# Six layer norms with ScalarE's square root and VectorE's reciprocal, and matmuls of the unit matrix in TensorE's waits

## The chip, the cores and the metric

The kernel runs on one core of a Trainium2 chip. The metric is the time of one execution on the device in microseconds. Three executions of the kernel before took 1084.04, 1086.39 and 1088.76 us (median 1086.39 us). One further execution was profiled.

## What is computed

Six layers work on a residual `x` of 2 x 1024 tokens with 128 channels. Each layer normalises `x` over its channels and adds its result to the residual:

```python
x = x + 0.5 * L0_ffn(layernorm(x))        # 4-bit quantised SwiGLU, FF = 352
x = x + L0_attn(layernorm(x))             # gated delta rule, 16 heads of 8
x = x + 0.5 * L0_ffn(layernorm(x))
x = x + 0.5 * L1_ffn(layernorm(x))        # shared expert + 1 of 8 experts, inner 256
x = x + L1_attn(layernorm(x))             # causal softmax attention
x = x + 0.5 * L1_ffn(layernorm(x))

def layernorm(x, eps=1e-05):
    m = jnp.mean(x, axis=-1, keepdims=True)
    v = jnp.var(x, axis=-1, keepdims=True)
    return (x - m) / jnp.sqrt(v + eps)
```

## The kernel before, in words

`build_program` (L2080) runs six stages one after the other: `fp4_ffn` (tag `_f1`), `delta_attention` (`_d`), `fp4_ffn` (`_f2`), `moe_ffn` (`_m1`), `causal_attention` (`_c`), `moe_ffn` (`_m2`). The names in the trace leave the number out, so both feed-forward stages show as `_f` and both expert stages as `_m`. Each stage consists of one or more blocks. In a block every engine has an instruction list of its own, written out by hand; lists are held together by semaphores (`wait_ge`), and at the end of a block all engines meet. An engine works through its list strictly in order, and whatever stands in front of a wait on an engine delays all that stands behind it.

**The norm (class `Norm`, L92).** The residual stays on chip as 16 tiles of 128 tokens x 128 channels. VectorE (DVE) takes the statistics of the 16 tiles (L112), works out the mean and the variance with epsilon (L115 to L121, each 128 x 16), and raises `s_var`. GpSimd (POOL) waits for it and raises the variance to the power -0.5, using a tile `halfpow` full of -0.5 (L128; in the attention stage the same instruction stands at L1787). It raises `s_rstd`; DVE has nothing to do until then, and after it subtracts and multiplies tile by tile (L134), raising `s_xn` for each tile. TensorE (PE) waits for these and turns each tile over: it multiplies it with the unit matrix `k.ident`.

**What follows the norm.** In `fp4_ffn` DVE and POOL quantise four tiles at a time (L162 to L174) and PE turns them afterwards (`turn_x`, L359), then `gate_up` (L368). In `transposed_norm` (L448, the first block of the delta stage with a norm) PE turns the 16 tiles (L469) and ScalarE (ACT) copies them out (L477); the block after it, `delta_inputs`, has its projections at L619 with a Silu on ACT at L650. In `moe_front` (L1213) PE turns four tiles (`turn`, L1270), ACT copies them out (L1328), PE computes the router's logits (`route`, L1276, 8 columns for each tile) and the shared expert's first product (`gate_up(0, 0)`, L1291), and behind that `count` (L1284). From the logits DVE finds the expert of each token (L1354 onwards) and its place in a sorted list; POOL scatters the rows into DRAM by 16 indirect transfers (L1261), and SP (the queue of transfers) reads them back in six loads (L1252). Meanwhile PE goes on with the shared expert (L1291, L1301).

`moe_routed` (L1406) is the next block. PE reads the expert numbers of the first two slots, and then for each of 24 slots turns the rows (`to_columns`, L1443), multiplies by the expert's weights (L1449, 512 columns), turns the hidden values (L1457) and multiplies again (L1465).

In `causal_attention` (L1648 onwards) POOL has its power in the middle of setting up constants: it comes after the memsets and before `V`'s ones (L1788), the selector `c_sel` (L1789) and the masks. PE turns the tiles (L1958) and projects q and k (L1966); ACT and DVE split them in bf16 parts, which SP sends to DRAM (L1730) and fetches back. At the end of this stage PE waits until DVE has the reciprocal of the softmax's denominators (`s_rec`, L1891), spreads it over the heads (L2066) and projects the result (L2074).

## Time and profile before

| | |
|---|---|
| median of three executions | 1086.39 us (1084.04 to 1088.76) |
| the profiled execution | 1078.19 us, of which the span from first to last instruction is 1076.5 us |
| PE busy | 736.8 us, 68% |
| DVE busy | 716.9 us, 67% |
| POOL busy | 411.6 us, 38% |
| ACT busy | 340.5 us, 32% |
| mean granted clock of PE | 0.855 of full |

No engine is busy all the time: the stages have different limits, and at the seams between them most engines stand idle in turn.
### The profile page before, as it was taken

The page shows a single profiled execution, that of the slowest core. Times are in us where ns is not written, and L with a number is a line of the kernel's source. Part 1 is how long each engine was busy: PE and PEld are TensorE (multiplying, and loading weights), DVE is VectorE, ACT ScalarE, POOL GpSimd, SP SyncE. Part 2 cuts the span into 40 slices and gives each one's busy share as a digit, 9 for nine tenths or more (in the row PEclk, how much of TensorE's full clock was granted, in tenths as well). Part 3 has the DMA queues.
Part 4 walks back from the last instruction along what each step waited for, and adds up shares of the span by engine and source line. Part 5 has one row for each costly group of instructions (what it writes and reads, how often), then busy time and mean ns, then how long its engine had stood idle before and what let it go on. Part 6 is the DMA issues. An engine that isn't in the chain of part 4 may idle for free. (4 is left out here: it accounts for less than half of the span.)

```text
span 1076.5 us, 15238 instructions
## 1 busy us (share of the span) xinstructions
PE 736.8 (68%) x5421; PEld 493.0 (46%) x5421; DVE 716.9 (67%) x1203; ACT 340.5 (32%) x579; POOL 411.6 (38%) x593
## 2 busy tenths in 40 slices
PE   0575145877775999836658792468787777738794
PEld 0354121477665998614455461233333333236462
DVE  7996484689996888389934234578887888244232
ACT  0211064000001550011211250417666666702152
POOL 3353100278886960034424254022333322302343
PEclk9987586689998999858958895759999999976897
DMA  7000000000000000030000212757100000000303
GB/s 180 0 1 1 11 0 0 1 1 1 2 1 1 2 2 1 15 117 1 1 0 31 79 41 73 244 97 114 28 8 9 8 9 8 7 3 13 89 32 106
DMA packets 42881, 35.89 MB, mean 33 GB/s; under 512 B 6167, under 2 KB 37336, under 8 KB 42808
## 3 DMA queue, kind: packets, MB, share of 16 engines
q1 hardware_dynamic: 40248, 29.61, 11.6%
q0 software_dynamic: 2560, 5.31, 1.5%
q8 instruction: 45, 0.74, 0.3%
q14 instruction: 28, 0.23, 0.1%
HBM read 17.45 MB, written 15.89 MB: 31 GB/s over the span
## 5 line engine op out<-in xcount | busy, mean ns | idle before, releaser
L1881 DVE TENSOR_REDUCE blockmax<-c_bank 128x8 f32<-128x1024 f32 x144 | 175.0, 1223 | 47.7 <-PE c_bank L2007 41.4
L1944 ACT ACTIVATE PT<-c_bank 128x1024 f32<-128x1024 f32 x144 | 145.5, 1025 | 71.8 <-PE c_bank L2029 71.7
L2043 PE MATMUL c_bank<-PT,V 128*9 128x256 f32 (+3 forms) x960 | 78.7, 431 | 14.5 <-POOL PT L1833 10.5
L798 PE MATMUL sums<-prod,ident 128*128 128x128 f32 x512 | 69.0, 293 | 27.0 <-DVE prod L824 27.0
L2000 PE MATMUL c_bank<-KA,QA 48*128 48x128 bf16 (+3 forms) x608 | 59.9, 282 | 36.0 <-DMA KA<-qk_parts_dram 16.2
L1833 POOL TENSOR_SCALAR_AFFINE_SELECT PT<-PT 128x256 f32<-128x256 f32 x128 | 49.1, 408 | 81.1 <-ACT PT L1944 81.0
L798 PEld LDWEIGHTS sums<-prod,ident 128*128 128x128 f32 x512 | 63.7, 203 | 32.2 <-DVE prod L824 32.2
L1539 POOL DMA_INDIRECT routed_results<-results_m,rows_m x48 | 46.0, 957 | 66.6 <-DVE results_m L1516 64.8
L2029 PE MATMUL c_bank<-QA,KA 51*128 51x128 bf16 (+3 forms) x480 | 56.8, 302 | 17.0 <-DMA QA<-nrows 16.5
L368 PE MATMUL gu_f<-gu_wT,xqT_f 128*128 128x352 f32 x128 | 52.8, 567 | 17.9 <-DVE h_f L298 17.9
L1522 DVE TENSOR_TENSOR r_h_m<-r_silu_m,r_gu_m 128x256 f32<-128x256 f32 x48 | 20.2, 421 | 66.9 <-ACT r_silu_m L1507 66.9
L1449 PE MATMUL r_gu_m<-m_gu,rowsT_m 128*128 x96 | 55.4, 661 | 1.8 <-ACT rowsT_m L1493 1.8
L754 POOL TENSOR_TENSOR decayed<-decayed,outer 128x512 f32<-128x512 f32 x32 | 40.6, 1269 | 32.8 <-DVE outer L843 32.8
L2000 PEld LDWEIGHTS c_bank<-KA,QA 48*128 48x128 bf16 x608 | 24.2, 97 | 59.5 <-ACT PT L1944 31.7
L171 POOL TENSOR_TENSOR q_yh_f<-q_yh_f,q_magich_f 128x704 f32<-128x704 f32 x16 | 26.8, 1676 | 60.7 <-DVE q_yh_f L168 57.1
L1261 POOL DMA_INDIRECT sorted_rows<-xs_m,where_m x32 | 31.0, 970 | 47.5 <-DVE where_m L1382 38.4
L783 ACT COPY s<-sums 128x64 f32<-128x64 f32 x32 | 6.8, 213 | 133.5 <-DVE wt L840 133.5
L368 PEld LDWEIGHTS gu_f<-gu_wT,xqT_f 128*128 128x128 f32 x128 | 28.9, 237 | 35.3 <-issue 28.5
L1815 POOL COPY negmax<-runmax 128x8 f32<-128x8 f32 x16 | 3.1, 193 | 108.6 <-DVE runmax L1886 108.6
L2043 PEld LDWEIGHTS c_bank<-PT,V 128*9 128x9 f32 x960 | 23.7, 90 | 43.6 <-issue 18.0
L2029 PEld LDWEIGHTS c_bank<-QA,KA 51*128 51x128 bf16 x480 | 16.3, 94 | 57.3 <-issue 28.4
L824 DVE TENSOR_TENSOR prod<-hist,keys 128x1024 f32<-128x1024 f32 x30 | 36.6, 1220 | 5.7 <-PE keys L790 3.0
(320 smaller groups left out, 1801.8 us busy)
## 6 DMA issues: line engine op xcount, KB each, us to landing
sorted_rows<-blank SPq DMA_DIRECT2D x2, 1584.0 KB, 14.0
rows_m<-sorted_rows SPq DMA_DIRECT2D x12, 264.0 KB, 4.7
qk_parts_dram<-qk_parts SPq DMA_DIRECT2D x8, 384.0 KB, 3.4
QA<-qk_parts_dram SPq DMA_DIRECT2D x6, 384.0 KB, 8.0
KA<-qk_parts_dram SPq DMA_DIRECT2D x6, 384.0 KB, 9.7
back_m<-routed_results SPq DMA_DIRECT2D x8, 256.0 KB, 3.7
qk_parts_dram<-qk_parts SPq DMA_DIRECT2D x8, 256.0 KB, 3.2
m_gu<-in_rt_gate SPq DMA_DIRECT2D x1, 1024.0 KB, 6.0
```

Source lines behind the costliest of these rows:

```text
L368: ins = nc.tensor.matmul(gu[:, s, m, 0:FF], xt, k.gu_wT[:, m * FF:(m + 1) * FF], start=True, stop=True)
L754: nc.gpsimd.tensor_tensor(decayed[:, kind], decayed[:, kind], outer1[:, kind], ALU.add).then_inc(s_added[kind], 1)
L798: ins = nc.tensor.matmul(sums[:, kind, 0], k.ident[:, :], prod[:, kind, e // HALF, :, e % HALF, :], start=(e == 0), stop=(e == DH - 1))
L824: nc.vector.tensor_tensor(prod[:, kind].rearrange("p a t e n -> p a t (e n)"), state.to_broadcast([P, 2, 2, HALF * NC]), keys[:, p % 2].re ...
L1449: nc.tensor.matmul(gu[:, j % 2, :], rowsT[:, j % 2, :], moe.gu[:, bass.ds(owner[j], 1), :], start=True, stop=True).then_inc(s_gu, 1)
L1539: nc.gpsimd.indirect_dma_start(out=result_dram[:, :], out_offset=bass.IndirectOffsetOnAxis(ap=rows[:, j, D:D + 1].bitcast(I32), axis=0), i ...
L1833: ins = nc.gpsimd.affine_select(out=diag, in_=diag, compare_op=ALU.is_ge, fill=0.0, base=0, pattern=[[0, BATCH], [1, P]], channel_multipli ...
L1881: nc.vector.tensor_reduce(blockmax[:, h % 2, :, HALFQ * n:HALFQ * (n + 1)], slot_of((1, m)).rearrange("p b (n c) -> p b n c", c=P), AX.X, ...
L1944: nc.scalar.activation(PT[:, u % PRING, :, :], slot_of((0, u)), ACT.Exp, scale=SCALE).then_inc(s_pt, 1)
L2000: ins = nc.tensor.matmul(out[:, b, n * P:end * P], QA[at, h, PLACE[i] * P:(PLACE[i] + 1) * P], KA[at, h, spot * P:(spot + end - n) * P], s ...
L2029: ins = nc.tensor.matmul(out[:, b, o:o + n], KA[at, h, PLACE[j] * P:(PLACE[j] + 1) * P], q, start=True, stop=True)
L2043: ins = nc.tensor.matmul(O[32 * g:32 * g + DH + 1, f * P:f * P + n], V[:, b, j, h, :], PT[:, u % PRING, b, o:o + n], start=(j == 0), stop= ...
```

## The change

It has two parts. First, in all six norms ACT takes the square root of the variance, after loading the table for it at the start of the block, and DVE takes the reciprocal; POOL's power and the tile `halfpow` are gone. Where another ACT table is needed afterwards it is loaded right behind the root (Silu in `fp4_ffn`, Sigmoid in `moe_front`). Second, `keep_busy` issues f32 matmuls of the unit matrix with itself (512 columns) into a bank of PSUM that is overwritten later. They wait for nothing and nothing waits for them: they stand in PE's list in front of work. There are 9 ahead of `turn_x(0, 0)` in `_f2`, 4 ahead of the turning in `_d`, 4 ahead of `turn(0)` and 2 behind the last `down` in the front of `_m1` and of `_m2`, 2 ahead of `to_columns(0)` in each routed block, 4 ahead of the wait for the weights in `_c`, and 9 ahead of its wait for `s_rec`: 42 in all.

```diff
+def keep_busy(k, bank, count):
+    for _ in range(count):
+        k.nc.tensor.matmul(bank, k.ident[:, :], k.ident[:, :].unsqueeze(1).to_broadcast([P, BANK // P, P]), start=True, stop=True)
...
-    def on_gpsimd(self, pool):
-        nc = self.nc
-        nc.gpsimd.memset(self.halfpow[:, :], -0.5).then_inc(self.s_half, 1)
-        pool.wait_ge(self.s_half, 1)
-        pool.wait_ge(self.s_var, 1)
-        nc.gpsimd.tensor_tensor(self.rstd[:, :], self.var[:, :], self.halfpow[:, :], ALU.pow).then_inc(self.s_rstd, 1)
+    def on_scalar(self, act):
+        act.preload_act_table(ACT.Sqrt)
+        act.wait_ge(self.s_var, 1)
+        self.nc.scalar.activation(self.std[:, :], self.var[:, :], ACT.Sqrt).then_inc(self.s_std, 1)
+
+    def on_vector_rstd(self, dve):
+        dve.wait_ge(self.s_std, 1)
+        self.nc.vector.reciprocal(self.rstd[:, :], self.std[:, :]).then_inc(self.s_rstd, 1)
...  fp4_ffn, TensorE and ScalarE
                 if prepare:
                     prepare.on_tensor(pe)
+                else:
+                    keep_busy(k, y[:, 0, :], 9)
                 turn_x(0, 0)
...
+                ln.on_scalar(act)
+                act.preload_act_table(ACT.Silu)
...  transposed_norm, TensorE
+                keep_busy(k, tp[:, 3, :], 4)
                 for t in range(TILES):
                     pe.wait_ge(ln.s_xn, t + 1)
...  moe_front, TensorE (start and end) and ScalarE
+                keep_busy(k, y[:, 0, :], 4)
                 turn(0)
...
+                keep_busy(k, logits[:, :], 2)
...
+                ln.on_scalar(act)
                 act.preload_act_table(ACT.Sigmoid)
...  moe_routed, TensorE
                 owner = {0: expert_of(0), 1: expert_of(1)}
+                keep_busy(k, y[:, 1, :], 2)
                 to_columns(0)
...  causal_attention, GpSimd
-                pool.wait_ge(s_set, 3)
-                pool.wait_ge(ln.s_var, 1)
-                nc.gpsimd.tensor_tensor(ln.rstd[:, :], ln.var[:, :], ln.halfpow[:, :], ALU.pow).then_inc(ln.s_rstd, 1)
                 nc.gpsimd.memset(V[:, :, :, :, DH:DH + 1].rearrange("p b j h a -> p (b j h a)"), 1.0).then_inc(s_set, 1)
...  causal_attention, TensorE
+                keep_busy(k, bank[:, 7, :], 4)
                 pe.wait_ge(s_w, 6 * 16)
                 turn_tiles(0)
...
+                keep_busy(k, bank[:, 4, :], 9)
                 pe.wait_ge(s_rec, 1)
```

## Rows read from the trace of the kernel before

**Rows 1.** Line 134, what ended its engine's idle time: us in total, times.
```profile
  POOL rstd_f L128: 6.2, 2
```
**Rows 2.** Timeline of all engines, front of `_m1`: start us, us, engine, line.
```profile
549.39 1.28 ACT L1325 ACT_TABLE_LOAD   x1 [4.27 <-PEq L85]
...
553.56 0.17 DVE L121 TENSOR_SCALAR var_m<-ln_tmp_m 128x16 f32<-128x16 f32 x1
553.88 2.90 POOL L128 TENSOR_TENSOR rstd_m<-var_m,halfpow_m 128x16 f32<-128x16 f32 x1 [4.38 <-DVE var_m L121]
556.82 4.19 DVE L134 TENSOR_SCALAR xn_m<-residual,mean_m,rstd_m 128x128 f32<-128x128 f32 x16 [3.09 <-POOL rstd_m L128]
...
557.22 2.27 PE L1270 MATMUL sh_gu_m<-ident,xn_m 128*128 128x128 f32 x8 [9.12 <-DVE xn_m L134]
558.50 0.59 ACT L1328 COPY xnT_m<-sh_gu_m 128x512 f32<-128x512 f32 x1 [7.83 <-PE sh_gu_m L1270]
```
**Rows 3.** Timeline of `_m1`: ACT takes a 128x16 function from DVE.
```profile
567.81 0.29 DVE L1354 TENSOR_REDUCE top_m<-logits_m 128x16 f32<-128x128 f32 x1 [6.81 <-PE logits_m L1276]
568.13 0.22 ACT L1330 ACTIVATE score_m<-top_m 128x16 f32<-128x16 f32 x1 [3.03 <-DVE top_m L1354]
```
**Rows 4.** Timeline of `_f1`: the smallest reciprocal on DVE.
```profile
22.56 0.35 DVE L164 RECIPROCAL q_invx_f<-q_scalex_f 128x32 f32<-128x32 f32 x1
```
**Rows 5.** Timeline of PE in `_m1`: router, then 512-column matmuls early and late.
```profile
564.27 3.42 PE L1276 MATMUL logits_m<-m_router,xnT_m 128*128 128x8 f32 x16
567.54 3.76 PE L1291 MATMUL sh_gu_m<-xnT_m,m_shared_gu 128*128 128x512 f32 x4
...
592.05 3.60 PE L1291 MATMUL sh_gu_m<-xnT_m,m_shared_gu 128*128 128x512 f32 x8
```
**Rows 6.** Timeline of PE in `_d`: the first work after 22.75 us of rest.
```profile
128.91 4.17 PE L469 MATMUL ntp_d<-ident,xn_d 128*128 128x128 f32 x16 [22.75 <-DVE xn_d L134]
```
**Rows 7.** Windows: stretch, length, busy us of PE, PEld, DVE, ACT, POOL, PEclk, DMA.
```profile
132.00:132.50 0.50, 0.50 (x4) 0.32 (x3) 0.50 (x3) 0.26 (x1) 0.00 (x0) 0.69 0.00 0
572.00:573.00 1.00, 1.00 (x3) 0.48 (x3) 0.77 (x3) 0.00 (x0) 0.00 (x0) 0.69 0.00 0
989.00:990.00 1.00, 1.00 (x6) 1.00 (x6) 0.73 (x4) 0.00 (x0) 0.70 (x2) 0.53 0.00 0
```
**Rows 8.** Timeline from the end of the front of `_m1` into its routed block.
```profile
597.05 2.05 PE L1301 MATMUL sh_y_m<-m_shared_down,sh_hT_m 128*128 128x128 f32 x16 [1.41 <-DVE sh_hT_m L1345]
597.52 3.13 SPq L1252 DMA_DIRECT2D rows_m<-sorted_rows  x6
...
602.64 0.33 PE L1443 MATMUL r_tpx_m<-ident,rows_m 128*128 128x128 f32 x1 [3.54 <-issue]
...
603.42 2.07 PE L1449 MATMUL r_gu_m<-m_gu,rowsT_m 128*128 x2 [0.45 <-ACT rowsT_m L1493]
...
611.23 1.06 PE L1449 MATMUL r_gu_m<-m_gu,rowsT_m 128*128 x2
...
612.91 1.06 PE L1449 MATMUL r_gu_m<-m_gu,rowsT_m 128*128 x2
```
**Rows 9.** Timeline of the front of `_c`: the norm, POOL's constants, first projections, first transfers.
```profile
668.29 5.50 DVE L134 TENSOR_SCALAR xn_c<-residual,mean_c,rstd_c 128x128 f32<-128x128 f32 x16 [3.13 <-POOL rstd_c L1787]
668.63 1.03 POOL L1789 COPY c_sel<-ident 128x1024 f32<-128x1024 f32 x1
...
671.79 3.53 PE L1966 MATMUL c_bank<-xnT_c,c_wqkv 128*128 128x512 f32 x4
...
677.46 17.72 SPq L1730 DMA_DIRECT2D qk_parts_dram<-qk_parts  x24
```
**Rows 10.** Timeline of PE at the end of `_c`.
```profile
950.75 5.76 PE L2066 MATMUL c_bank<-c_rec,c_sel 128*128 128x256 f32 x16 [9.34 <-DVE c_rec L1891]
...
956.35 0.83 PE L2074 MATMUL c_bank<-c_wp,YT 128*128 128x128 f32 x6
```
**Rows 11.** Timeline of PE in `_f2`: its first work.
```profile
469.09 1.11 PE L359 MATMUL htp_f<-ident,xq_f 128*128 128x128 f32 x4 [16.70 <-POOL xq_f L174]
```

More of the change, by code:

```diff
@@ L101, in __init__ @@
         self.rstd = k.sb(f"rstd{tag}", [P, TILES], ctx=ctx)
-        self.halfpow = k.sb(f"halfpow{tag}", [P, TILES], ctx=ctx)
+        self.std = k.sb(f"std{tag}", [P, TILES], ctx=ctx)
         self.xn = xn if xn is not None else k.sb(f"xn{tag}", [P, TILES, D], ctx=ctx)
         self.s_var = k.sem(f"s_var{tag}")
-        self.s_half = k.sem(f"s_half{tag}")
+        self.s_std = k.sem(f"s_std{tag}")
         self.s_rstd = k.sem(f"s_rstd{tag}")
@@ L310, in _ @@
                 ln.on_vector_stats(Chain(dve, s_ldve))
+                ln.on_vector_rstd(dve)
                 ln.on_vector_apply(dve, 0, XTILES)
@@ L343, in _ @@
                     moe.on_gpsimd(k, pool)
-                ln.on_gpsimd(pool)
                 for g in range(XG - 1):
@@ L458, in _ @@
                 ln.on_vector_stats(Chain(dve, s_dve))
+                ln.on_vector_rstd(dve)
                 ln.on_vector_apply(dve)
-            @block.gpsimd
-            def _(pool):
-                ln.on_gpsimd(pool)
             @block.tensor
             def _(pe):
+                keep_busy(k, tp[:, 3, :], 4)
                 for t in range(TILES):
@@ L1256, in _ @@
             def _(pool):
-                ln.on_gpsimd(pool)
                 pool.wait_ge(s_xs, 2)
@@ L1321, in _ @@
                             gate_up(c + 1, half)
+                keep_busy(k, logits[:, :], 2)
             @block.scalar
             def _(act):
+                ln.on_scalar(act)
                 act.preload_act_table(ACT.Sigmoid)
@@ L1391, in _ @@
                 ln.on_vector_stats(Chain(dve, s_ndve))
+                ln.on_vector_rstd(dve)
                 ln.on_vector_apply(dve)
@@ L1775, in _ @@
                 nc.gpsimd.memset(ones[:, :], 1.0).then_inc(s_ones, 1)
-                nc.gpsimd.memset(ln.halfpow[:, :], -0.5).then_inc(s_set, 1)
                 nc.gpsimd.memset(zeros[:, :], 0.0).then_inc(s_set, 1)
@@ L1790, in _ @@
                     [P, DH, HEADS, DH])).then_inc(s_set, 1)
-                pool.wait_ge(s_set, 5)
+                pool.wait_ge(s_set, 4)
                 for n, base in enumerate((0, HALFP, -HALFP)):
@@ L1796, in _ @@
                                             pattern=[[-1, P]], channel_multiplier=1).then_inc(s_set, 1)
-                pool.wait_ge(s_set, 11)
+                pool.wait_ge(s_set, 10)
                 for n, t in enumerate((idm, future)):
@@ L1801, in _ @@
                         nc.gpsimd.tensor_copy(t[at, s, :], shifted[at, 3 * n + shift, :]).then_inc(s_set, 1)
-                pool.wait_ge(s_set, 19)
                 def add_bias():
@@ L1849, in _ @@
                 ln.on_vector_stats(Chain(dve, s_ldve))
+                ln.on_vector_rstd(dve)
                 ln.on_vector_apply(dve)
@@ L1866, in _ @@
                 low(NQK - 1)
-                dve.wait_ge(s_set, 4)
+                dve.wait_ge(s_set, 3)
                 for g in range(4):
@@ L1912, in middle @@
                     nc.scalar.copy(parts[:, n % RING, 1, :], rest[:, n % RING, :]).then_inc(s_mid, 1)
+                ln.on_scalar(act)
                 act.wait_ge(s_w, 6 * 16)
@@ L1982, in _ @@
                 pe.wait_ge(s_rest, NQK)
-                pe.wait_ge(s_set, 19)
+                pe.wait_ge(s_set, 18)
                 def group_of(h):
```

## The prediction

> **What bounds the kernel now.** I read the page's share of busy time first: PE 68% and DVE 67%, so nothing bounds the whole, and the seams have to be read one by one. Then what ended the idle time ahead of line 134: POOL's power does, twice for 6.2 us in all in the feed-forward stages [rows 1]. Three more lines of that answer hold the other four norms with 3.1 us each. So at six seams DVE stands still for 3.1 us, and the timeline of one seam shows that all others stand still with it: PE's first turn comes 0.40 us after DVE's first tile, with 9.12 us of rest before it [rows 2]. Last come the windows with PEclk. In `_m1` PE rests through the norm, then works from 557.22 us, and the clock rises to full only within 572 to 573 us [rows 2, 7]. In that time it works at half speed on the way to the experts' choice. The same holds in the front of `_c`, at its end, and in the routed blocks.
>
> **Part 1, the norms.** Removed from each seam: the 3.12 us between the variance's end and the first tile (3.09 to 3.13 in the rows) [rows 1, 2, 9]. Added: a hand-over from DVE to ACT, 0.03 us (568.10 to 568.13), and a 128x16 function, 0.22 us, a Sigmoid standing in for the root [rows 3]; a hand-over back, taken as 0.03 us as well; the reciprocal of 128x16, at most the 0.35 us of the 128x32 one, at least the 0.17 us of the 128x16 instruction before the power, and I take 0.25 us as half the elements lie between [rows 2, 4]; and DVE's own wait for it, 0.04 us. That is 0.57 us, with bounds 0.45 and 0.8 us. Each seam gains 2.55 us, six gain **15.3 us** (13.9 to 16.0). Nothing else is late at the variance: PE, ACT and POOL wait for this chain.
>
> The table loads of the root stand at the block's start, where the Sigmoid's load stood: 1.28 us from 549.39, done long before the variance at 553.73 [rows 2]. The second load moves behind the root. In `_m` the root ends 0.32 us ahead of the first tile, the load 0.96 us behind it, and ACT's first copy came 1.68 us behind it: hidden by 0.7 us [rows 2]. If that cover were gone it would cost up to 1.28 us in each `_m` and less in the others. The Trainium skill ("ScalarE: Activation LUTs", What ACT_TABLE_LOAD costs) gives 2.66 us for every switch with its drain; by that the copy would be 0.66 us late in each `_m`, 1.3 us in the sum. No row here shows a drain.
>
> In `_c` POOL no longer holds its constants back until the power is done. The 16 tiles took 5.50 us there against 4.19 us in `_m`, because the 1.03 us copy of `c_sel` ran beside the first one [rows 2, 9]. It now runs beside the statistics: **1.2 us** (0 to 1.3).
>
> **Part 2, what a matmul of the unit matrix costs.** Its kind is L1291, 512 columns in f32. Four records, that is two matmuls, take 3.76 us at 1.2 GHz, and eight records, four matmuls, 3.60 us at 2.4 GHz [rows 5]; without the tail of the last, 1.71 and 0.86 us each. All 42 are 72 us cold and 36 us warm, so almost all must lie under waits. What they bring is clock. Whether they raise it: two dense cold matmuls and little more raised it in `_m1` (from 567.54 to within 572 to 573) [rows 5, 7]. A start at block begin should therefore be warm after some 3 to 5 us.
>
> The four ahead of the norm's turns (`_d`, `_m1`, `_m2`, `_c`) have 549.39 to 557.22 less 2.55, that is 5.28 us of cover [rows 2]. With two cold and two warm they take 5.1 us: hidden. All cold they take 6.84 us and overrun by 1.56 us. What the clock then gives:
> - `_d`: nothing; DVE paces the turns at 0.26 us, and the clock is full before the projections anyway [rows 6, 7].
> - `_m` fronts: from 557 us to the counts come 32 router records (16 of them in 3.42 us [rows 5], so 6.84 us) and two cold matmuls of 512 columns. At full clock throughout, 3.4 and 1.7 us go, 5.1 us. At the least nothing does. The question is whether the clock stays up through work of 8 columns: in `_m1` this work, cold and unbroken, did not raise it [rows 5, 7], and in `_m2` the clock fell within 989 to 990 us with PE busy throughout, after a short rest [rows 7]. I take it to hold for the first part only and to be lost before the last 16 records: 1.7 us, nearer the row that fell. Two stages: **3.4 us** (0 to 10.2).
> - `_c` front: the first two projections are dense and come at once; they go from 1.71 to 0.86 us each, and SP's transfers, which run without a break from 677.46 us for 17.7 us, start that much sooner [rows 9]: **1.7 us** (0 to 1.8).
>
> The nine in `_f2` have until 469.09 less 2.55; PE has rested since 452.39 (16.70 us before), and with some 2 us for the meeting of the engines that leaves 12 us of cover, of which a run half cold takes 10 [rows 11]. What follows there is a chain on DVE with a turn only now and then; I count 0 (0 to 0.7).
>
> The nine at the end of `_c` have 9.34 us [rows 10]. PE comes out of the heads' work at 2.4 GHz, so they take 7.7 us and keep it. The eight matmuls at L2066 took 950.75 to 956.35, 5.6 us, and take 8 x 0.43 = 3.4 us warm: **2.2 us** (0 to 2.2).
>
> The two pairs around the experts' seam are the doubtful ones. PE's last work in the front ended at 599.10, SP's issues at 600.65 [rows 8]. A warm pair ends at 600.81 and holds the block back by 0.2 us; a cold one to 602.52, by 1.9 us. The pair ahead of `to_columns(0)` stands plainly on the path, since PE's rest before the first turn is put down to its own issue and not to a transfer [rows 8]: 1.7 us warm, 3.4 us cold. It buys the first three slots at full clock: 603.42 to 611.23 is 7.81 us against three times 1.68 us (611.23 to 612.91), 2.8 us [rows 8]. Net 2.8 - 1.7 - 0.2 = 0.9 us in each, **1.8 us** (minus 7 to plus 2).
>
> **The sum.** 15.3 + 1.2 + 3.4 + 1.7 + 2.2 + 1.8 = 25.6 us. The profiled execution took 1078.19 us (span 1076.5, 1.7 around it), so it would come to 1052.6 us. That execution was 8.2 us faster than the median of the three shown; I take the same difference off the median: 1086.4 - 25.6 = 1060.8, rounded to **1061 us**.
>
> **The rivals.**
> *The clock holds through the fronts.* The `_m` fronts give 5.1 us each in place of 1.7: 6.8 us more, 1054 us. For it: PE no longer rests there. Against it: the fall at 989 us.
> *The clock is lost again before the work.* The matmuls then only cost. The norms' 15.3, 1.2 for `c_sel` and 2.2 at the end of `_c` stay; the experts' seams cost 2 x (2.5 + 0.2): 13.3 us, 1073 us. For it: at that seam PE still rests, from the first pair's end to the second pair, for some 1.9 us. In `_d` 16 plain turns raised the clock within 132.0 to 132.5 us, with PE at rest for 22.75 us before [rows 6, 7]. The Trainium skill ("TensorE: Matmul & The Clock Gate", Part 4) says that turning does not count as busy for the clock; by that rule every front would lose its clock during the turns, as this rival has it. The row of `_d` disagrees, so I give the rival no more than a fifth.
> *Slower than before: the matmuls stay cold and overrun their waits.* At a price p each, the overruns are 4 x (4p - 5.28) ahead of the turns, 2 x (2p - 1.55) behind the fronts, 4p in the routed blocks and 9p - 9.34 at the end of `_c`, that is 33p - 33.5. At p = 1.71 it is 22.9 us, against 16.5 us from the norms and `c_sel`: 1093 us. It decides from p = 1.51 us on. Against it: dense matmuls raised the clock wherever they ran for 5 us.
> *The root's chain is no shorter.* If the table load came behind the wait for the variance, 1.28 us would stand in each chain: 7.7 us less gain, 1069 us. Against it: the Sigmoid's preload ran at block start [rows 2].
>
> **How the numbers follow.** Forecast 50%, clock holds 19%, clock lost 22%, slower 4%, root's chain 5%. The range of 1051 to 1074 us takes in all but the slower case and the tails of the two outer ones. A change of 0.5% is 5.4 us, about what a measurement of this kernel can tell from none. Faster by more: 93%; within: 3%; slower: 4%.
>
> **What would show it.** ACT's root and DVE's reciprocal within 0.6 us between variance and first tile, six times; table loads at block starts. In `_m`, PEclk 1.00 in the turns and 0.50 before the last router records (lost) or 1.00 up to the counts (holds). In the routed block, L1449 at 1.68 us from the first slot, and its first turn 1.9 us later after SP's last issue than before. At the end of `_c`, L2066 in 3.5 us. Wrong at once: unit-matrix records of 0.85 us in the routed block, a PE still on them when the first tile is ready, or a gap of 3 us left ahead of line 134.

## The result, and the profile after

| | before | after | ratio |
|---|---|---|---|
| median | 1085.28 us (four executions) | 1058.30 us (four executions, 1056.38 to 1061.64) | 0.9749, 95% interval 0.9722 to 0.9777 |
| profiled execution | 1078.19 us, span 1076.5 | 1056.38 us, span 1054.7 | |

The forecast was 1061 us, 25.6 us less than before. The medians differ by 27.0 us, the two profiled executions by 21.8 us. Why these two numbers disagree turned out to be a question of its own (below).

The page of the changed kernel: busy time of each engine, and PE's granted clock in forty slices.

```profile
span 1054.7 us, 15405 instructions
...
PE 762.8 (72%) x5505; PEld 498.4 (47%) x5505; DVE 717.7 (68%) x1209; ACT 349.2 (33%) x591; POOL 392.9 (37%) x581
...
PEclk9987687699997999877969997759999999997997
```

PE is busy for 26.0 us longer than before and the kernel is over 20 us shorter. The clock's mean rose from 0.855 to 0.887.

The norm's chain in `_m1`, from the timeline of all engines (start us, us, engine, line; it answers to [rows 2]):

```profile
539.17 1.28 ACT L130 ACT_TABLE_LOAD   x1 [4.28 <-PEq L85]
...
539.20 5.89 PE L95 MATMUL sh_y_m<-ident 128*128 128x512 f32 x8 [1.33 <-PEq L85]
...
543.34 0.17 DVE L127 TENSOR_SCALAR var_m<-ln_tmp_m 128x16 f32<-128x16 f32 x1
543.55 0.21 ACT L132 ACTIVATE std_m<-var_m 128x16 f32<-128x16 f32 x1 [3.10 <-DVE var_m L127]
...
543.78 1.28 ACT L1338 ACT_TABLE_LOAD   x1
543.80 0.25 DVE L136 RECIPROCAL rstd_m<-std_m 128x16 f32<-128x16 f32 x1 [0.28 <-ACT std_m L132]
...
545.62 0.58 ACT L1341 COPY xnT_m<-sh_gu_m 128x512 f32<-128x512 f32 x1 [0.56 <-PE sh_gu_m L1280]
```

From the variance's end (543.51) to the first tile (544.09) it is 0.58 us, where it was 3.09 us [rows 2]. The table of the next function is loaded behind the root, ends at 545.06, and the copy comes 0.56 us later: hidden. The reciprocal of 128x16 takes 0.25 us. All six norms look like this (0.57 us each).

PE in the same stretch, then its granted clock (windows: stretch, length, busy us of PE, PEld, DVE, ACT, POOL, PEclk, DMA):

```profile
544.93 1.68 PE L1280 MATMUL sh_gu_m<-ident,xn_m 128*128 128x128 f32 x8
...
549.02 2.17 PE L1286 MATMUL logits_m<-m_router,xnT_m 128*128 128x8 f32 x16
551.04 3.38 PE L1301 MATMUL sh_gu_m<-xnT_m,m_shared_gu 128*128 128x512 f32 x4
```
```profile
542.00:543.00 1.00, 1.00 (x3) 0.48 (x2) 0.93 (x8) 0.00 (x0) 0.00 (x0) 0.50 0.00 0
543.00:544.00 1.00, 1.00 (x2) 0.32 (x2) 0.65 (x5) 0.43 (x2) 0.00 (x0) 0.67 0.00 0
544.00:545.00 1.00, 1.00 (x4) 0.40 (x3) 0.96 (x5) 1.00 (x1) 0.00 (x0) 1.00 0.00 0
...
548.00:550.00 2.00, 2.00 (x21) 2.00 (x20) 0.27 (x2) 1.11 (x2) 0.00 (x0) 1.00 0.04 8
550.00:552.00 2.00, 2.00 (x9) 1.52 (x10) 0.62 (x3) 0.35 (x2) 0.00 (x0) 0.62 0.00 0
552.00:554.00 2.00, 2.00 (x4) 0.93 (x3) 1.93 (x5) 1.15 (x1) 0.00 (x0) 0.52 0.02 4
554.00:556.00 2.00, 2.00 (x9) 1.04 (x8) 1.97 (x4) 0.60 (x1) 0.00 (x0) 1.00 0.00 0
```

The clock comes up before the first turn and stays up through all turns and nearly all router records (2.17 us for 16, before 3.42 [rows 5]). It falls at 550.5 us, as the dense products begin, with PE busy since 539.20 us. PE goes from the multiplications into the turns without a rest.

To locate gains and losses I cut all executions at the same rows and took the differences of their starts. Each column is one profiled execution in us; "changed" is the kernel just shown, after_again the same kernel on another chip, before_again the kernel before on that chip; the others are the experiments below. R is the first row of DVE that reads `psR`, behind the delta stage's scan. The stretches between those of the table are left out, so the rows don't add up to the span. The longest of them, in `_c` from SP's first store to `c_rec`, took 271.5 to 275.3 us, in an order that doesn't go with the edits.

| from, to | before | before_again | norms_only | busy_only | changed | after_again | seam_moved | best |
|---|---|---|---|---|---|---|---|---|
| start, first tile of `_f1` | 20.47 | 20.20 | 17.79 | 20.29 | 17.84 | 17.75 | 18.07 | 17.72 |
| first tile of `_d`, R | 219.64 | 217.41 | 221.91 | 220.10 | 216.27 | 219.08 | 219.75 | 219.02 |
| R, first tile of `_f2` | 113.56 | 113.50 | 110.95 | 113.50 | 110.94 | 110.96 | 111.02 | 110.95 |
| `_m1`: first tile, router's maxima | 10.99 | 10.98 | 10.99 | 10.91 | 7.22 | 7.41 | 7.29 | 7.10 |
| `_m1`: SP's loads of rows, first turn of rows | 5.12 | 5.17 | 7.88 | 13.42 | 10.16 | 7.16 | 5.82 | 6.31 |
| `_m1`: first turn of rows, SP's loads of results | 50.72 | 52.12 | 50.59 | 47.86 | 47.87 | 47.96 | 48.88 | 48.39 |
| `_c`: first tile, SP's first store | 9.17 | 8.24 | 8.33 | 9.33 | 6.58 | 6.60 | 6.58 | 6.60 |
| `c_rec`, first tile of `_m2` | 20.32 | 20.68 | 17.38 | 18.28 | 15.77 | 15.78 | 15.77 | 15.78 |
| `_m2`: first tile, router's maxima | 10.99 | 10.99 | 10.99 | 10.91 | 10.93 | 6.95 | 10.92 | 6.94 |
| `_m2`: SP's loads of rows, first turn of rows | 5.97 | 4.92 | 8.38 | 11.14 | 11.18 | 7.03 | 5.37 | 5.38 |
| `_m2`: first turn of rows, SP's loads of results | 50.66 | 50.81 | 50.54 | 47.99 | 47.94 | 47.98 | 47.98 | 47.88 |
| span | 1076.5 | 1075.2 | 1066.4 | 1083.5 | 1054.7 | 1046.5 | 1052.8 | 1044.4 |

### The profile page after: what moved, and what is told of

Its sections match the earlier page's. It is cut to its first block and busy times, and to the rows that moved or that the text cites. A ratio compares the mean times of both kernels' runs of the same rounds, so it can differ in the third digit from the quotient of the medians.

```text
span 1054.7 us, 15405 instructions
## 1 busy us (share of the span) xinstructions
PE 762.8 (72%) x5505; PEld 498.4 (47%) x5505; DVE 717.7 (68%) x1209; ACT 349.2 (33%) x591; POOL 392.9 (37%) x581
## 5 line engine op out<-in xcount | busy, mean ns | idle before, releaser
L376 PE MATMUL gu_f<-gu_wT,xqT_f 128*128 128x352 f32 x128 | 50.5, 546 | 17.9 <-DVE h_f L306 17.8
L1463 PE MATMUL r_gu_m<-m_gu,rowsT_m 128*128 x96 | 50.3, 605 | 2.2 <-ACT rowsT_m L1508 2.2
L2042 PEld LDWEIGHTS c_bank<-QA,KA 51*128 51x128 bf16 x480 | 16.4, 94 | 57.0 <-issue 28.2
L393 PE MATMUL y_f<-down_wT,hqT_f 128*128 128x128 f32 (+1 forms) x192 | 30.8, 320 | 13.2 <-ACT hqT_f L431 13.2
```

The source lines that it names most:

```text
L376: ins = nc.tensor.matmul(gu[:, s, m, 0:FF], xt, k.gu_wT[:, m * FF:(m + 1) * FF], start=True, stop=True)
L1463: nc.tensor.matmul(gu[:, j % 2, :], rowsT[:, j % 2, :], moe.gu[:, bass.ds(owner[j], 1), :], start=True, stop=True).then_inc(s_gu, 1)
L2042: ins = nc.tensor.matmul(out[:, b, o:o + n], KA[at, h, PLACE[j] * P:(PLACE[j] + 1) * P], q, start=True, stop=True)
```

## The experiments

They ran in three groups of four, each group on one chip with the kernel before beside it. The medians of the kernel before on these chips were 1083.95, 1077.36 and 1078.33 us, so kernels of different groups are compared by their ratios.

### First group: the two parts alone, the pairs, and _m2's front

**norms_only**, all seven calls of `keep_busy` removed from the changed kernel, of which one is shown:

```diff
...
-                keep_busy(k, y[:, 0, :], 4)
...
```

> The changed kernel without any multiplication of the unit matrix: its norms (ACT's root, DVE's reciprocal) and the new order of the constants in _c stay. Theory A (the sum of the prediction, its terms checked on the trace after): six norms at 2.54 us and 1.1 us for the copy of c_sel, 16.4 us less than before, ratio 0.985; the clock at the fronts, the end of _c and in the routed blocks as before. Rival B: most of the gain comes from the shorter chains, with the clock following by itself from PE's shorter rests; then 20 us or more, ratio 0.981 or less. On the late ACT function in the shared expert (a rest of 7.14 us ahead of the last pair of Silus in _m1, some 2.5 us more than the pace asks): theory A puts it down to ACT's longer program, so it is here as well; if it comes from PE's added instructions it is absent here. The 3.8 us that the delta stage gave between 160 and 212 us without any edit in it: if they hang on how far the stages' start is shifted against the clock, they can be here in any size, and no theory forecasts them.

Measured: 1067.26 us, ratio 0.9846 (0.9831 to 0.9861), 16.7 us less. Theory A forecast 16.4 us. The table shows the norms alone: 2.7 us at `_f1`, 2.6 us at `_f2`, and the fronts of `_m1` and `_m2` at 10.99 us as before. The clock doesn't follow by itself, so rival B falls. The profile of this kernel has the late Silus told of below, which is part of why it is only 10.1 us shorter than that of the kernel before.

**busy_only**, the kernel before plus the same seven calls:

```diff
...
+                keep_busy(k, y[:, 0, :], 4)
                 turn(0)
...
```

> The kernel before with all 42 multiplications of the unit matrix and none of the rest: GpSimd's power stays, with the order of _c's constants. Theory A: the multiplications give what the after trace shows of them, some 4 in the front of _m1, 1 to 2 in _m2's, 1.8 in _c's front, 2.0 at the end of _c, less 0.7 in each routed block's seam: 7 to 8 us less than before, ratio 0.993; the norms' chains take 3.12 us as before, and ACT's Silus in the shared expert keep the pace they had before (no 7 us rest). Rival C (the rests of PE are 2.5 us longer here than in the changed kernel, so the clock is lost again between multiplications and turns): ratio 0.998 or more, with a granted clock of 0.50 in the router's records of both _m stages.

Measured: 1088.17 us, ratio 1.0038 (1.0022 to 1.0053): 4.2 us *slower* than before. Theory A (7 to 8 us faster) falls, and rival C holds in a stronger form. The fronts of `_m1`, `_m2` and `_c` take what they took before. PE in the front of `_m1`, and its clock:

```profile
549.99 6.53 PE L95 MATMUL sh_y_m<-ident 128*128 128x512 f32 x8 [1.33 <-PEq L85]
557.79 2.27 PE L1279 MATMUL sh_gu_m<-ident,xn_m 128*128 128x128 f32 x8 [1.27 <-DVE xn_m L140]
```
```profile
557.00:558.00 1.00, 0.21 (x1) 0.14 (x1) 0.61 (x3) 0.00 (x0) 0.35 (x1) 1.00 0.00 0
558.00:559.00 1.00, 1.00 (x5) 0.55 (x4) 1.00 (x5) 0.08 (x1) 0.00 (x0) 1.00 0.00 0
559.00:560.00 1.00, 1.00 (x6) 0.74 (x5) 1.00 (x6) 0.51 (x1) 0.00 (x0) 0.58 0.00 0
```

GpSimd's power holds the first tile back, PE rests for 1.27 us, and the clock falls some 1.4 us behind the first turn, before it has bought anything. In the changed kernel the shorter norm closes that rest. That the rest is what loses the clock is argued from this pair of profiles and not shown: further down, a rest of 1.6 us in `_m2` lost it in some executions and not in others. At `_m1`'s experts' seam the clock was down as well: the last `down` took 3.79 us (2.05 before), the pair behind it 2.91 us, and the first turn of rows came 13.4 us behind SP's loads. What did pay is 2.0 us at the end of `_c` and 2.9 and 2.7 us in the routed blocks. The rows name where 4.2 us can be lost; they don't add up to exactly that number, because no profile of the kernel before exists from this chip.

**no_seam_pairs**, the two pairs around the experts' seam removed:

```diff
-                keep_busy(k, logits[:, :], 2)
...
-                keep_busy(k, y[:, 1, :], 2)
```

> The changed kernel without the two pairs at the experts' seams (2 at the front's end, 2 ahead of the first turn of rows, in each _m). The prediction had the pairs bring 0.9 us net in each stage: by that this kernel is 1.8 us slower than the changed one. Theory A (the trace after): each pair stands on the path with 1.7 to 1.9 us, 3.5 us in all, and they bring 2.8 us of pace in the first three slots: this kernel is 0.8 us faster in each stage, 1.6 us in all, and its first turn of rows comes 3.5 us sooner behind PE's last matmul of the shared expert (5.4 us now, 1.9 to 3.5 us here), with the first three slots at 2.6 us apart as before. If ACT's late Silu in the shared expert is still there (rest of 7 us), it doesn't come from these pairs.

Measured: 1060.80 us, ratio 0.9790 (0.9768 to 0.9813). In its `_m1` the first turn of rows comes 7.89 us behind SP's loads (10.16 in the changed kernel), but from there to the loads of results it takes 50.60 us (47.87). So the pairs cost 2.3 us there and bring 2.7 us, 0.4 us net where Silus are late. In its `_m2` the turn comes only 0.7 us sooner (10.44 against 11.18) and the block takes 2.6 us longer (50.54 against 47.94), 1.9 us net. Theory A had 3.5 us for the cost and falls; in time the pairs can't be told from nothing here.

**m2_six**, six multiplications in `_m2`'s front, with `out` handed on to `moe_front`:

```diff
-                keep_busy(k, y[:, 0, :], 4)
+                keep_busy(k, y[:, 0, :], 6 if out is not None else 4)
```

> The changed kernel with six instead of four multiplications ahead of the turns in _m2 alone (_m1 keeps four). In the changed kernel the four ran warm there, ended 1.6 us ahead of the first turn, and the clock fell at the first turns and stayed at 0.50 for 14 us; in _m1, where the four ran cold and PE had no rest before its turns, it stayed full until the router was nearly done. Theory A (the rest loses the clock): with six there is no rest, the clock holds through most of the router as in _m1, and the span from first normalised tile to the router's maxima falls from 10.9 to about 7.2 us: 3.7 us faster than the changed kernel, ratio to before 0.9715. Rival B (the turns and the 8-column matmuls lose it, whenever they come): the clock falls within 2 us of the same place, and the time is the changed kernel's within 0.5 us.

Measured: 1057.87 us, ratio 0.9780 (0.9755 to 0.9805). First tile to maxima took 8.96 us: the clock fell 4.4 us behind the first tile, where it fell 1.3 us behind it in the changed kernel, not at the same place as rival B has it, and theory A's 7.2 us wasn't reached either. The third group settles how much this says.

### The late Silus

In all four kernels of this group, and in the changed kernel as first profiled, ACT comes late near the end of the shared expert, with nothing waited for that the trace shows. The changed kernel:

```profile
573.38 0.60 ACT L1348 ACTIVATE sh_silu_m<-sh_gu_m 128x512 f32<-128x512 f32 x1 [1.12 <-PE sh_gu_m L1301]
...
580.38 3.13 SPq L1263 DMA_DIRECT2D rows_m<-sorted_rows  x6
581.13 1.08 ACT L1348 ACTIVATE sh_silu_m<-sh_gu_m 128x512 f32<-128x512 f32 x2 [7.14 <-PE sh_gu_m L1301]
```

The rest should be 4.58 us; it is 7.14 us, and the function comes 0.75 us behind SP's first load. In the kernel before the last Silu (595.68) is earlier than that load (597.52). PE's last `down` and the whole seam are late with it. The next two kernels ask whether the edit does this.

### Second group

**small_ones**, the kernel before with 42 matmuls of one column ahead of `_f2`'s turns:

```diff
+                else:
+                    for _ in range(42):
+                        nc.tensor.matmul(y[:, 0, 0:1], k.ident[:, :], k.ident[:, 0:1], start=True, stop=True)
                 turn_x(0, 0)
```

> The kernel before with 42 matmuls of one column each (unit matrix times its first column) in PE's wait ahead of _f2's turns: as many instructions as the change adds to PE, some 0.05 to 0.1 us each, far too short to bring the clock up or to overrun that wait. Asks where the late Silus of the shared expert come from: all four kernels run so far show ACT's 5th and 7th Silu late in both _m stages, the 7th only 0.8 to 1.5 us behind SP's first load of rows, so 3 to 4 us late; the kernel before doesn't. Theory D (the place of the code: what comes later in the program lies elsewhere, and ACT's instructions arrive late there): the late Silus appear here too, and the time is 2 to 5 us above before's. Rival E (something the multiplications or the norms do in the _m stages themselves): Silus at before's pace, first load of rows 1.7 us or more behind the last Silu, time that of before within 1 us.

Measured: 1078.17 us, ratio 1.0001 (0.9986 to 1.0015), and no late Silu. Their price was mis-sized: 84 records took 18.05 us, 0.21 us each and two to a matmul. They did overrun the wait: the first turn came 10.49 us behind the first tile, 7.38 us before. The next wait swallowed it, for `gate_up` began at 14.84 us behind that tile, as before. Theory D would fall, but nothing in this whole group had a late Silu, so the run says less than it should.

**late_scatter**, the changed kernel with POOL's scatters held back:

```diff
                 pool.wait_ge(s_where, 1)
+                pool.wait_ge(s_silu, NB * HALVES)
```

> The changed kernel with GpSimd's sixteen scatters held back until ACT's eighth Silu is done, so that no scatter runs beside the shared expert. Asks whether the scatters make ACT late. If they do (ACT's late instructions come over the same transfer engines): Silus 5 to 8 keep the pace of 1.7 and 5.2 us by turns, with the last some 14 us behind the third; the kernel as a whole is some 14 to 20 us slower in each _m, because the rows are loaded later. If not: a rest of ACT of 7 us and more with nothing waited for stays ahead of the last pair, at the same place in its program.

Measured: 1094.60 us in one execution. The Silus keep their pace, and the loads of rows come 50.3 us behind the maxima in place of 29.1, so 21 us later in each `_m` and not 14 to 20. Since no kernel of this group was late, it doesn't show that the scatters are the cause. It stays open.

**no_d_f2**, without the four in `_d` and the nine in `_f2`:

```diff
-                    keep_busy(k, y[:, 0, :], 9)
...
-                keep_busy(k, tp[:, 3, :], 4)
```

> The changed kernel without the four multiplications in _d and without the nine in _f2; the other 29 stay. The prediction counted both at nothing: then this kernel's time is the changed kernel's (ratio to before 0.975). Rival F (the four in _d shift PE's clock in the delta stage: three executions with them gained 0.5 to 3.4 us between the first normalised tile of _d and the end of the scan, the two with the norms alone or with the old norms lost 0.5 to 2.3 us): 3 to 5 us slower than the changed kernel, ratio 0.978 to 0.980, with the loss between 160 and 350 us. The nine in _f2 give nothing in either.

Measured: 1055.67 us, ratio 0.9790 (0.9764 to 0.9817). By the ratio that is where rival F puts it. By the rows it isn't: from the first tile of `_d` to R it took 217.65 us, inside the range of kernels that have the four (216.3 to 219.8).

**seam_moved**, the same two pairs at other places:

```diff
                 for c in range(NB):
+                    if c + 1 == NB:
+                        keep_busy(k, logits[:, :], 2)
                     down(c)
...
-                keep_busy(k, logits[:, :], 2)
...
+                keep_busy(k, y[:, 1, :], 2)
                 owner = {0: expert_of(0), 1: expert_of(1)}
-                keep_busy(k, y[:, 1, :], 2)
```

> The changed kernel with its two pairs at the experts' seam moved, none removed: the pair on logits goes ahead of the shared expert's last down (where PE waits 2.9 us for ACT and DVE), the pair on y goes ahead of the two loads of expert numbers into PE's registers, not behind them. Theory A (each pair stood on the path with 1.7 to 1.9 us, and the register loads of 1.9 us run beside matmuls that are already issued): first turn of rows 3.5 us sooner after PE's last matmul of the shared expert (2 to 3.5 us in place of 5.4), pace of 1.68 us from the first slot kept: 2.5 to 3.5 us faster in each _m, 5 to 7 us in all, ratio 0.969. Rival G (PE's rest behind the block's end loses the clock, or the register loads wait for the matmuls anyway): the y pair still delays the turn by its own 1.7 us; 2 us faster or less.

Measured: 1049.91 us, ratio 0.9727 (0.9698 to 0.9756). PE at the seam of its `_m1`:

```profile
584.10 1.95 PE L1311 MATMUL sh_y_m<-m_shared_down,sh_hT_m 128*128 128x128 f32 x16
588.00 2.45 PE L95 MATMUL r_y_m<-ident 128*128 128x512 f32 x4 [1.95 <-PEq L1258]
590.24 0.42 PE L1458 MATMUL r_tpx_m<-ident,rows_m 128*128 128x128 f32 x1
```

The first turn comes 4.19 us behind the last `down` (5.42 us in no_d_f2, where the pairs have their old places), and in `_m2` 3.44 us. The register loads do run beside the pair. Against SP's loads the gain is 1.2 and 1.7 us. In `_m1` 1.0 us of it goes again, because the clock fell during the pair (48.88 us in the routed block instead of 47.9). So the truth lies between theory A and rival G.

### Third group: the same kernels on one chip

**after_again** and **before_again** are the two kernels unchanged, so they have no diff.

> The changed kernel as it is, on the same chip as the next three, to read them against it. Also for the late Silus: they showed in all four kernels of one group of runs and in none of the four of another, so neither the norms nor the multiplications decide it. If they go with the chip, all four of this group show them in both _m stages or none does; if with the kernel, this one shows them (it did in its first profile) and no_d_f2, which differs from it before _m1 alone, does not. Ratio to before 0.975 to 0.979. First normalised tile to the router's maxima 7.2 us in _m1 and 10.9 in _m2, in _c first tile to SP's first store 6.6, first turn of rows to SP's first load of results 47.9 us.

> The kernel before as it is, for one more profile. Its profile shown at the start took 1078 us where its timed runs took 1084 to 1089, and on two other chips its median was 1084 and 1077 us. If the late Silus go with the chip, they are here exactly when the other three of this group have them, with the first turn of rows 7.9 us behind SP's first load in place of 5.1, and a time 5 to 6 us above 1077; if they go with the kernel, they are absent here whatever the others show.

Measured: after_again 1048.20 us, ratio 0.9731 (0.9704 to 0.9758); before_again 1076.94 us in one execution. No Silu was late in any of the four, and the changed kernel is among them. Its ratio is just outside the 0.975 to 0.979 expected, because `_m2`'s front took 6.95 us and not 10.9. The same program had late Silus on one chip and none on another, so the edit by itself doesn't bring them; they go with the chip or with what a group shares. Whether the kernel before has them on those chips too, no profile shows. Where changed kernels showed them, the median of the kernel before was 1085.28 and 1083.95 us; where they didn't, 1077.36 and 1078.33. They cost 2.8 us in `_m1` and at least 2.4 us in `_m2` (7.88 and 8.38 us in norms_only against 5.12 and 5.97 us; before_again took 4.92 us in `_m2`, which makes it 3.5). It fits that the timed runs of before had them too and its profiled execution didn't, which would explain 21.8 us in the profiles against 27.0 in the medians. No profile of the kernel before shows them, so this stays an inference. On this chip the profiles differ by 28.7 us (1075.2 - 1046.5) and the medians by 30.1 us.

**no_d**, without the four in `_d` alone:

```diff
-                keep_busy(k, tp[:, 3, :], 4)
```

> The changed kernel without the four multiplications in _d; the nine in _f2 stay. Forecast of the prediction: nothing, ratio equal to after_again's within its interval. Rival F (they shift PE's clock in the delta stage): 3 us or more slower than after_again, lost between 160 and 350 us. Against F so far: from the first normalised tile of _d to the first carry behind the scan five profiles with the four took 216.3 to 219.8 us, the two with new norms without them 217.7 and 221.9, so that a difference of the two means of 2 us stands beside a spread of 3.5 us.

Measured: 1052.64 us, ratio 0.9745 (0.9720 to 0.9771), 4.4 us above after_again with overlapping intervals. In the profile `_d` to R took 221.32 us. Seven profiles of changed kernels with the four took 216.3 to 219.8 us (mean 218.0), busy_only 220.1; the three changed kernels without them took 217.7, 221.3 and 221.9 us. That leans to rival F with some 2 us, but executions of the kernel before, also without them, took 217.4, 218.1 and 219.6 us. The scatter is as large as the effect: not settled.

**best**, the edits of seam_moved and m2_six together:

```diff
-                keep_busy(k, y[:, 0, :], 4)
+                keep_busy(k, y[:, 0, :], 6 if out is not None else 4)
...
+                    if c + 1 == NB:
+                        keep_busy(k, logits[:, :], 2)
                     down(c)
...
-                keep_busy(k, logits[:, :], 2)
...
+                keep_busy(k, y[:, 1, :], 2)
                 owner = {0: expert_of(0), 1: expert_of(1)}
-                keep_busy(k, y[:, 1, :], 2)
```

> The changed kernel with the two pairs moved (as in seam_moved) and six multiplications ahead of _m2's turns (as in m2_six). From the rows of those two: 1.2 to 1.9 us at each experts' seam (first turn of rows 5.4 to 5.8 us behind SP's first load instead of 7.0 where no Silu is late), up to 1 us lost again in a stage whose clock falls during the y pair, and 2.0 us in _m2's front (9.0 us in place of 10.9): 3 to 5 us less than after_again, ratio to it 0.995 to 0.997. If the gains are swallowed by what is late next, its time is after_again's.

Measured: 1046.39 us, ratio 0.9703 (0.9687 to 0.9719), the fastest kernel of all. The seams gave 0.9 and 1.7 us against after_again (6.31 and 5.38 against 7.16 and 7.03). `_m2`'s front gave nothing: 6.94 us with six against 6.95 with four. 1.8 us between the medians, with overlapping intervals, is less than the 3 to 5 us expected. In the profile of after_again the four already did what six were meant to do.

That makes `_m2`'s front the most instructive stretch. The same four multiplications, ending 1.61 us ahead of the first turn both times; first the changed kernel, then after_again:

```profile
944.00:946.00 2.00, 0.45 (x2) 0.28 (x2) 1.61 (x9) 1.37 (x2) 0.00 (x0) 1.00 0.00 0
946.00:948.00 2.00, 2.00 (x10) 1.48 (x9) 2.00 (x10) 0.85 (x3) 0.00 (x0) 0.61 0.00 0
948.00:950.00 2.00, 2.00 (x11) 2.00 (x11) 1.34 (x6) 0.45 (x1) 0.00 (x0) 0.50 0.00 0
...
958.00:960.00 2.00, 2.00 (x5) 0.97 (x4) 1.97 (x1) 0.39 (x1) 0.00 (x0) 0.50 0.00 0
960.00:962.00 2.00, 2.00 (x6) 0.73 (x5) 1.50 (x6) 0.20 (x1) 0.00 (x0) 0.98 0.00 0
```
```profile
944.00:946.00 2.00, 0.39 (x3) 0.16 (x2) 1.58 (x9) 1.20 (x2) 0.00 (x0) 1.00 0.00 0
946.00:948.00 2.00, 2.00 (x12) 1.30 (x11) 2.00 (x9) 1.00 (x3) 0.00 (x0) 1.00 0.00 0
948.00:950.00 2.00, 2.00 (x20) 2.00 (x21) 1.52 (x6) 1.06 (x2) 0.00 (x0) 1.00 0.00 0
950.00:952.00 2.00, 2.00 (x20) 2.00 (x19) 0.00 (x0) 0.59 (x1) 0.00 (x0) 1.00 0.00 0
952.00:954.00 2.00, 2.00 (x5) 0.96 (x5) 1.58 (x7) 1.38 (x2) 0.00 (x0) 0.61 0.00 0
954.00:956.00 2.00, 2.00 (x7) 1.18 (x6) 2.00 (x1) 0.72 (x2) 0.00 (x0) 0.54 0.00 0
956.00:958.00 2.00, 1.83 (x5) 0.52 (x4) 1.83 (x8) 0.14 (x1) 0.00 (x0) 1.00 0.00 0
```

In the one the clock falls among the turns at about 946.4 us and stays down for nearly 14 us; in the other it falls at 952.4 us, when the dense matmuls begin, and is back 3.4 us later. That is 4.0 us of difference with one and the same program. So a rest of 1.6 us doesn't lose the clock every time. It may still make it likelier: of the seven profiles with four multiplications and this rest, the clock fell within 0.9 to 1.5 us of the first turn in five, after 3.8 us in no_d and after 6.7 us in after_again; in the two with six and no rest (m2_six and best) it fell after 4.0 and 6.5 us. What six bring over four stays open.

## Why the prediction was right, point by point

| term of the sum | forecast us | measured us | from |
|---|---|---|---|
| six norms | 15.3 | 15.2 | 2.52 to 2.56 in each, between variance and first tile, changed against before |
| `c_sel` in `_c` | 1.2 | 1.1 of DVE, 0.8 of the front | 16 tiles in 4.40 us instead of 5.50; first tile to SP's first store 9.17 to 8.33, before to norms_only |
| fronts of `_m` | 3.4 | 3.8, and 7.6 on the third chip | 10.99 to 7.22 in `_m1`; 10.99 to 10.93 or 6.95 in `_m2`, each to the router's maxima |
| front of `_c` | 1.7 | 1.7 | 8.33 to 6.6, norms_only to changed |
| `_f2` | 0 | 0 | 110.95 us with and without |
| `_d` | 0 | 0 to 2 | not settled |
| end of `_c` | 2.2 | 1.6 to 2.0 | 17.38 to 15.77; 20.32 to 18.28 |
| experts' seams | 1.8 | 1.4 without late Silus; minus 4.7 in the changed kernel's own profile | 2.0 us later, 2.7 us shorter, twice; 5.0 and 5.2 us later, 2.9 and 2.7 us shorter |

The terms don't add up to the two differences measured, and part of the agreement is luck. Between the two first profiles the stretches give 15.2 for the norms, 4.6 for the fronts of `_m` down to SP's loads of rows, 2.6 for the front of `_c` with `c_sel`, 2.0 for its end and minus 4.7 for the seams: 19.7 us. The delta stage gave another 3.4 us (219.64 to 216.27) for which the prediction has no term, and 1.3 us went elsewhere, which makes the 21.8 us. The medians moved by 27.0 us, and no profile shows which stretches made up the difference.

*The norms.* Right in every part: the chain is 0.58 us (0.57 forecast), the reciprocal 0.25 us, the table loads are hidden, and norms_only measured 16.7 us against 16.5 for the first two terms.
The Trainium skill ("ScalarE: Activation LUTs", What ACT_TABLE_LOAD costs) gives 2.66 us for a switch with its drain. The rows disagree. In the changed kernel the Silu's load in `_d` was followed straight away by the function:

```profile
129.75 1.28 ACT L661 ACT_TABLE_LOAD   x1 [0.26 <-PEq L467]
131.04 1.42 ACT L661 ACTIVATE pad<-proj,d_bias 128x512 f32<-128x512 f32 x2
```

The 1.3 us that this figure would have cost in the two `_m` stages didn't appear.

*The fronts.* The mechanism was right, its size was the step that was off. I let the clock go before the last 16 router records; in `_m1` it held through almost all of them, fell at 550.5 us and came back after 3.4 us, so that all nine executions with the changed front gave 3.4 to 3.9 us there, not 1.7. The term was meant down to the counts, and there `_m1` gave 4.6 us (15.34 to 10.78 us behind the first tile). `_m2` took the lower bound in the profiled execution, so that the sum came out at 3.8 against 3.4: two errors of opposite sign. On the third chip both fronts gave, and the kernel came out nearer to the rival "the clock holds".
The Trainium skill ("TensorE: Matmul & The Clock Gate", Part 4) says that turning doesn't count as busy. In `_d` of the kernel before the clock rose during 16 turns [rows 6, 7], which speaks against it. The fronts don't decide it: in the nine of `_m1` the full clock outlasted all 16 turns, but it fell 1.3 to 2.2 us behind the last of them, and in seven of the nine of `_m2` it fell before the last turn.

*The front of `_c`.* The two terms on it don't simply add up. The norms' kernel without multiplications gained 0.8 us of the 1.1 that DVE gained, and before_again reached SP's first store in 8.24 us without either part, because its clock rose 1.9 us sooner against the first tile. Together they gave 2.6 us against the first profile and 1.6 us on the third chip, 2.9 forecast.

*The experts' seam.* The prediction put the pair ahead of the turn at 1.7 us and the pair behind the front at 0.2 us, and counted 2.8 us for the first slots. after_again (no late Silu):

```profile
581.72 2.05 PE L1311 MATMUL sh_y_m<-m_shared_down,sh_hT_m 128*128 128x128 f32 x16 [1.41 <-DVE sh_hT_m L1358]
582.16 3.12 SPq L1263 DMA_DIRECT2D rows_m<-sorted_rows  x6
...
583.61 1.88 PE L95 MATMUL logits_m<-ident 128*128 128x512 f32 x4
...
587.50 1.98 PE L95 MATMUL r_y_m<-ident 128*128 128x512 f32 x4 [2.02 <-issue]
...
589.32 0.27 PE L1457 MATMUL r_tpx_m<-ident,rows_m 128*128 128x128 f32 x1
```

SP's issues end at 585.28 us and the first pair at 585.49, 0.2 us later; the turn comes 4.04 us behind SP's end, 1.99 before [rows 8], so 2.05 us are lost against 1.9 forecast. The routed block is 2.7 us shorter. It holds where the Silus are on time. Where they are late, PE's `down` is the last to come, and the first pair stands on the path as well: 2.3 us lost and 0.4 us net in `_m1`.

*The rivals.* "The clock is lost again before the work" had 22%. It isn't what the changed kernel does in `_m1` and `_c`, but it is what happened in `_m1` to the multiplications without the shorter norm (busy_only, 1088 us), and in `_m2` of the changed kernel's first profile. That the two parts depend on each other was missing from the prediction: it used the shorter norm only as less cover for the multiplications and added the two up. By the ratios they would give -1.5% and +0.4% apart, and give -2.5 to -2.7% together. These come from different chips; on the chip of the two parts only the variants without the pairs and with six ran, at -2.1 and -2.2%. "No shorter chain" fell at once, and the matmuls didn't stay cold. The argument against that last rival, that dense matmuls raised the clock wherever they ran for 5 us, was wrong as it stands. In the delta stage of the kernel before, 16 records of 512 columns that read 8 partitions ran without a rest for 14.02 us and the clock stayed down:

```profile
185.90 14.02 PE L641 MATMUL sums<-norm,from_row 8*128 8x512 f32 x16 [4.50 <-DVE norm L691]
```
```profile
188.00:194.00 6.00, 6.00 (x8) 2.35 (x8) 3.91 (x4) 0.00 (x0) 0.00 (x0) 0.50 0.00 0
```

*The base.* Taking the forecast off the median and not off the profiled execution turned out closer: 1078.19 less 25.6 would have given 1052.6 us, 6 us too low for that chip.

## What to carry to other kernels

Warming matmuls can cost more than they bring: 42 of them alone made this kernel 0.4% slower, and with the waits behind them shortened they brought time. So shorten the wait first, then fill it, and measure the two together as well as apart. They needn't reach right up to the work everywhere. At the end of `_c` the nine ended 1.4 us ahead of it, and the clock stayed full in all ten profiles that have them:

```profile
921.77 7.99 PE L95 MATMUL c_bank<-ident 128*128 128x512 f32 x18
...
931.18 3.72 PE L2080 MATMUL c_bank<-c_rec,c_sel 128*128 128x256 f32 x16 [1.42 <-DVE c_rec L1902]
```

Here they cost less in front of register loads than behind them, and where the engine waits anyway than behind its last work in a block. Before a few microseconds are put down to an edit, look at the same stretch in several executions of the same program: the clock alone moved one stretch by 4.0 us.

## What the runs showed of the hardware that I had not expected

- PE's clock fell while PE was busy, and how long it stayed down differed: 3.4 us at 1.2 GHz when it fell as dense matmuls began (after_again, 952.4 us), 13.7 us when it fell among turns and router records (changed kernel, 946.4 us).
- ACT's last two Silus of a block came some 2.5 to 4 us late, 0.75 to 1.5 us behind SP's first load of rows in most cases, with nothing in the trace that they waited for. It was so in every profile of five kernels and in none of the nine others (one of them the same program as one of the five). Its cause wasn't found; the shift of the median of before between chips, 6 to 8 us, is of the size of two such delays.
- A matmul of one column against the 128x128 unit matrix took 0.21 us for each of its two records at 1.2 GHz (small_ones, 84 records in 18.05 us), where I had put in 0.05 to 0.1 us for the whole matmul.
